# A four-stage graph network on one core: ScalarE's order in the plain layer, and the order and fusing of the last round

## The reference

```
# stage 1, "plain layer" (G = adjacency with multiplicities)
h = max(layernorm(x), 0)
t = (h + G h) W1 + b1;  t = relu(batch_norm(t));  x = x + relu(t W2 + b2)
h = max(layernorm(x), 0)                     # input of stage 2

# stage 3: h = max(layernorm(x),0) W_in + b_in, then four times (i = 0..3)
agg = norm * (G + I) (h Wc[i]) + bc[i]
y   = h + relu(agg)
mu  = mean(y);  var = mean((y - mu)^2)
h   = (y - mu) * rsqrt(var + 1e-5) * ln_g[i] + ln_b[i]
# after the fourth: out = x + h
```

## Time and profile before

| | |
|---|---|
| median of 3 runs | 2899.14 us (2898.2 to 2923.24) |
| span of the profiled execution, first to last instruction | 2555.2 us |
| plain layer, first to last sum matmul of its own | 1178.98 to about 1247 us |
| four last layers | about 2231 to 2544.8 us |
| last store issued | 2545.20 us |

### The profile page before, as it was taken

The page is one execution under the profiler, slowest core; times in us unless marked ns, Lnnn a source line. Parts: engine busy times, 40 slices in busy tenths (PEclk is TensorE's granted clock), DMA queues, the critical chain, the costliest instruction groups (busy, mean ns, idle before and its releaser), DMA issues.

```text
span 2555.2 us, 33445 instructions
## 1 busy us (share of the span) xinstructions
PE 1957.3 (77%) x11712; PEld 1075.9 (42%) x11712; DVE 1320.5 (52%) x3185; ACT 672.7 (26%) x1332; POOL 1480.3 (58%) x1529
## 2 busy tenths in 40 slices
PE   8855544554455544438999999999999999999996
PEld 4411111111111111125556555555555565577775
DVE  6576666666766666654322222222323333367775
ACT  4354454554445444424300000000000000100000
POOL 5477777777777777771166666664676667500000
PEclk8765565656565656568999999999999999999998
DMA  6655555555555555565454444445444444400000
GB/s 205 194 161 167 159 167 161 167 161 164 160 168 164 165 164 166 162 213 184 140 187 160 163 157 155 154 153 171 147 153 152 142 162 159 126 32 1 1 6 22
DMA packets 183330, 370.17 MB, mean 145 GB/s; under 512 B 38760, under 2 KB 119254, under 8 KB 174838
## 3 DMA queue, kind: packets, MB, share of 16 engines
q1 hardware_dynamic: 129208, 263.74, 29.1%
q0 software_dynamic: 48704, 101.21, 15.3%
q10 hardware_dynamic: 5246, 3.03, 0.4%
HBM read 232.54 MB, written 135.28 MB: 144 GB/s over the span
## 4 chain that ended last, share of the span: by engine, by line
PE 49%; DVE 3%; ACT 1%; issue 1%; DMA 0%; SPq 0%; ACTq 0%
PE ps_out L1910 26%; PE ps_out L1272 11%; PE ps_out L1890 6%; PE ps_out L1866 4%; PE ps_t L1343 1%; DMA bias<-in_L_gnn_ln_b 0%; DVE arena L1655 0%; PE ps_t L1840 0%; PE ps_out L1331 0%; PE ps_out L1880 0%; ACT H L875 0%; ACT H L882 0%; DVE H L1510 0%; DVE CS L1500 0%; DVE H L1511 0%
## 5 line engine op out<-in xcount | busy, mean ns | idle before, releaser
L946 POOL DMA_INDIRECT arena<-table_rel,key_rel x784 | 778.1, 992 | 245.5 <-issue 234.8
L1620 POOL DMA_INDIRECT arena<-table_cut,src_at x324 | 312.0, 963 | 256.2 <-DMA table_cut<-Z 103.2
L1063 PE MATMUL ps_t<-arena 128*128 128x50 f16 x1568 | 96.6, 213 | 462.1 <-DVE arena L975 462.1
L965 DVE SCALAR_TENSOR_TENSOR arena<-arena,keep_max 128x128 f32<-128x128 f32 x784 | 274.6, 350 | 322.6 <-DMA arena<-table_rel,key_rel 309.7
L1620 POOL DMA_INDIRECT arena<-table_next,src_at x324 | 315.5, 974 | 179.0 <-issue 91.8
L1128 ACT ACTIVATE arena<-ps_out 128x800 fp8e4<-128x800 f32 x512 | 399.9, 835 | 44.3 <-PE ps_out L1076 44.2
L1076 PE MATMUL ps_out<-arena 128*128 128x400 f16 x1024 | 375.0, 503 | 43.2 <-ACT arena L1128 43.2
L1910 PE MATMUL ps_out<-arena,Z 128*128 128x512 fp8e4 x1600 | 350.6, 379 | 0.9 <-DVE Z L868 0.9
L1910 PE MATMUL ps_out<-arena,cut 128*128 128x512 fp8e4 x1600 | 350.2, 379 | 0.0
L1063 PEld LDWEIGHTS ps_t<-arena 128*128 128x128 f16 x1568 | 79.2, 116 | 542.7 <-DVE arena L975 523.6
L981 DVE TENSOR_TENSOR arena<-iota,arena 128x1072 f16<-128x1072 f16 (+1 forms) x384 | 271.4, 707 | 0.0
(11 more groups left out here) (313 smaller groups left out, 2026.3 us busy)
## 6 DMA issues: line engine op xcount, KB each, us to landing
arena<-adjacency SPq DMA_DIRECT2D x64, 1600.0 KB, 6.9
adjacency<-arena SPq DMA_DIRECT2D x160, 320.0 KB
running_rows<-arena SPq DMA_DIRECT2D x392, 128.0 KB
arena<-adjacency_plain SPq DMA_DIRECT2D x50, 400.0 KB, 7.5
arena<-table_rel,key_rel POOLq DMA_INDIRECT x784, 2.9
table_rel<-arena SPq DMA_DIRECT2D x13, 512.0 KB, 3.9
adjacency_plain<-adj SPq DMA_DIRECT2D x50, 128.0 KB, 2.4
table_rel<-adj SPq DMA_DIRECT2D x12, 512.0 KB, 3.9
```

Of the source, the lines that this page charges most:

```text
L946: e.indirect_dma_start(message(g, t), None, table, bass.IndirectOffsetOnAxis(key[:, t:t + 1], 0)).then_inc(s_msg[t % both], 16)
L965: e.scalar_tensor_tensor(fold(t), fold(t - 1), g.keep_max[:, t:t + 1], message(g, t), ALU.add, ALU.max).then_inc(s_run, 1)
L1063: e.matmul(out[:, :, w * WIN:(w + 1) * WIN], g.hot_low[:, q % 2, w // 2, :, w % 2], g.hot_flat[:, q % 2, w // 2, :, w % 2].rearrange("p (a ...
L1620: e.indirect_dma_start(g.picked[:, w % 2 * BLOCKS + k, :, :].rearrange("p a f -> p (a f)"), None, tables[y], bass.IndirectOffsetOnAxis(g.s ...
```

## The change

1. In the plain layer ScalarE does `m.scalar` of rounds 0 and 1 first, then `norm.scalar` of rounds 0 and 1. Rounds 2 to 4 stay as they were.
2. In the last round of the last layer TensorE sums the three-tile part, then the first 6 of 25 source tiles (`AHEAD`) of the two-tile part, then multiplies the three-tile part by the weights, then sums the other 19 source tiles and multiplies the two-tile part.
3. In that round VectorE and ScalarE work on the three-tile part and on the two-tile part one after the other (`last_part`): ScalarE takes the squares of (y - mean) and their sums, and VectorE's centring, gain, scaling, shift and add to X become one fused operation per tile for (y - mean) * gain, one per tile for the scaling and the add to X, and one add of the shift to X ahead of both parts.
4. The last stores are three tiles after the first part, one tile and the 53 rows after the second.

```diff
@@ class Sums
+    def tensor_last(self, e, i, cut, weights, base):
+
+        n = base * (2 * TROUNDS)
+        e.wait_ge(self.s_z, n + (2 * i - 2))
+        e.sem_inc(self.s_go, 1)
+        self.add(e, i, 0, cut, range(NT), True, True).then_inc(self.s_sum, 1)
+        self.add(e, i, 1, cut, range(AHEAD), True, False)
+        self.product(e, i, 0, weights, n)
+        self.add(e, i, 1, cut, range(AHEAD, NT), False, True).then_inc(self.s_sum, 1)
+        self.product(e, i, 1, weights, n)
...
@@ isomorphism_layer
     def scalar(e):
         batch_norm_scalar(g, e, s_v, s_r)
-        for i in range(TROUNDS):
+        for i in range(EARLY_ROUNDS):
+            m.scalar(e, i, 1.0 / (scale * COUNT))
+        for i in range(EARLY_ROUNDS):
+            norm.scalar(e, i)
+        for i in range(EARLY_ROUNDS, TROUNDS):
             m.scalar(e, i, 1.0 / (scale * COUNT))
             norm.scalar(e, i)
@@ graph_layers, sync
-        for i in range(TROUNDS):
-            e.wait_ge(s_fin, i + 1)
-            lo, hi = i * TILES, min((i + 1) * TILES, NT - 1)
+        for done, lo, hi in [(r + 1, r * TILES, (r + 1) * TILES) for r in range(TROUNDS - 1)] + [
+                (TROUNDS + 2, NT - TILES, NT - 2), (TROUNDS + 4, NT - 2, NT - 1)]:
+            e.wait_ge(s_fin, done)
@@ graph_layers, vector
+        def last_part(q):
+
+            n, i, (lo, hi) = 3, TROUNDS - 1, m.parts[q]
+            at = slice(i * TILES + lo, i * TILES + hi)
+            y, h, var = g.Y[:, at, :], g.H[:, at, :], g.var[:, at]
+            e.wait_ge(m.s_prod, n * (2 * TROUNDS) + (2 * i + q + 1))
+            e.tensor_tensor(y, m.out(q).rearrange("p (k f) -> p k f", f=D),
+                            g.dis[:, at].unsqueeze(2).to_broadcast([P, hi - lo, D]), ALU.mult).then_inc(m.s_read, 1)
+            e.wait_ge(m.s_read, n * (2 * TROUNDS) + (2 * i + q + 1))
+            step(e.tensor_tensor(y, y, g.w9[:, (4 + n) * D:(5 + n) * D].unsqueeze(1).to_broadcast([P, hi - lo, D]), ALU.add))
+            step(e.scalar_tensor_tensor(y, y, 0.0, h, ALU.max, ALU.add))
+            step(e.tensor_reduce(g.mean[:, at], y, AX.X, ALU.add))
+            e.tensor_scalar(g.mean[:, at], g.mean[:, at], -1.0 / D, None, ALU.mult).then_inc(s_mean, 1)
+            e.wait_ge(s_mean, q + 1)
+            for k in range(at.start, at.stop):
+                e.scalar_tensor_tensor(g.H[:, k, :], g.Y[:, k, :], g.mean[:, k:k + 1], g.bias9[:, n * D:(n + 1) * D],
+                                       ALU.add, ALU.mult).then_inc(s_add, 1)
+            e.wait_ge(s_sq, hi)
+            e.tensor_scalar(var, var, 1.0 / D, 1e-5, ALU.mult, ALU.add).then_inc(s_v, 1)
+            e.wait_ge(s_r, ended + q + 1)
+            step(e.reciprocal(g.inv_dev[:, at], g.dev[:, at]))
+            e.wait_ge(s_add, hi + 1)
+            for k in range(at.start, at.stop):
+                e.scalar_tensor_tensor(g.X[:, k, :], g.H[:, k, :], g.inv_dev[:, k:k + 1], g.X[:, k, :],
+                                       ALU.mult, ALU.add).then_inc(s_fin, 1)
+
...
+                if n == 3 and i == TROUNDS - 1:
+                    tail = slice(i * TILES, NT)
+                    e.tensor_tensor(g.X[:, tail, :], g.X[:, tail, :], tall(g.bias9[:, (4 + n) * D:(5 + n) * D]),
+                                    ALU.add).then_inc(s_add, 1)
+                    e.wait_ge(s_add, 1)
+                    for q in range(2):
+                        last_part(q)
+                    continue
@@ graph_layers, scalar
+        def last_round(n, i):
+            m.mean(e, i, 0, g.inverse[:, n:n + 1], n)
+            squares(0)
+            m.mean(e, i, 1, g.inverse[:, n:n + 1], n)
+            deviation(0)
+            squares(1)
+            deviation(1)
```

More of the change, by code:

```diff
@@ L78 @@
 TILES = 5
+AHEAD = 6
 TROUNDS = NT // TILES
@@ L1324, in tensor, with mean, product @@
         self.products(e, i, weights, base)
+    def tensor_last(self, e, i, cut, weights, base):
[7 more added lines that the diff above has]
+        self.product(e, i, 1, weights, n)
+    def mean(self, e, i, q, inverse, base):
+        n, (lo, hi) = base * (2 * TROUNDS), self.parts[q]
+        e.wait_ge(self.s_prod, n + (2 * i - 2))
+        e.wait_ge(self.s_sum, n + (2 * i + q + 1))
+        e.sem_inc(self.s_go, 1)
+        e.activation(self.z[:, i % 2, lo * P:hi * P], self.sums(i, q), ACT.Copy, scale=inverse).then_inc(self.s_z, 1)
+    def product(self, e, i, q, weights, n):
+        lo, hi = self.parts[q]
+        e.wait_ge(self.s_z, n + (2 * i + q + 1))
+        e.wait_ge(self.s_read, n + (2 * i - 1 + q))
+        for k in range(lo, hi):
+            last = e.matmul(self.out(q)[:, (k - lo) * D:(k - lo + 1) * D], self.z[:, i % 2, k * P:(k + 1) * P],
+                            weights, start=k == lo, stop=k == hi - 1)
+        last.then_inc(self.s_prod, 1)
     def products(self, e, i, weights, base=0):
@@ L1456, in graph_layers @@
     s_c, s_v, s_r, s_fin, s_o = g.sem("gchain"), g.sem("gvar"), g.sem("gdev"), g.sem("gfinal"), g.sem("gout")
+    s_mean, s_sq, s_add = g.sem("gendmean"), g.sem("gendsquare"), g.sem("gendshift")
+    ended = 4 * TROUNDS - 1
     cuts = (g.zcut, g.cut)
@@ L1524, in scalar, with squares, deviation @@
     def scalar(e):
+        def squares(q):
+            lo, hi = m.parts[q]
+            e.wait_ge(s_mean, q + 1)
+            for k in range(lo, hi):
+                at = NT - TILES + k
+                e.activation(T[:, k, :], g.Y[:, at, :], ACT.Square, bias=g.mean[:, at:at + 1],
+                             accum_out=g.var[:, at:at + 1]).then_inc(s_sq, 1)
+        def deviation(q):
+            at = slice(NT - TILES + m.parts[q][0], NT - TILES + m.parts[q][1])
+            e.wait_ge(s_v, ended + q + 1)
+            e.activation(g.dev[:, at], g.var[:, at], ACT.Sqrt).then_inc(s_r, 1)
+        def last_round(n, i):
[5 more added lines that the diff above has]
+            deviation(1)
         def layer(n, x):
@@ L1527, in layer @@
                 at = slice(i * TILES, (i + 1) * TILES)
+                if n == 3 and i == TROUNDS - 1:
+                    last_round(n, i)
+                    continue
                 m.scalar(e, i, g.inverse[:, n:n + 1], base=n)
@@ L1548, in layer @@
                     e.wait_ge(s_last, 16 * TILES)
+                if n == 3 and i == TROUNDS - 1:
+                    m.tensor_last(e, i, cuts[x], g.w9[:, n * D:(n + 1) * D], n)
+                    continue
                 m.tensor(e, i, cuts[x], g.w9[:, n * D:(n + 1) * D], base=n, parts_of=parts_of if n else None)
```

## The result

| | before | changed |
|---|---|---|
| median of 10 runs each | 2899.22 us | 2884.88 us |
| lowest to highest | 2888.56 to 2923.24 | 2872.47 to 2897.81 |
| ratio | | 0.9954, 95% interval 0.9932 to 0.9975 |
| profiled execution: time, span | not given, 2555.2 | 2877.94, 2874.3 |

The change is worth 14.3 us at the medians, 7 to 20 us by the interval: within 1% of no change, and 1.1 us from the forecast of 2886.0.

The account below looks back on a forecast made before the run. Mostly TensorE bounds, idle behind ScalarE's order in the plain layer, with VectorE's chain alone at the end; 8.5 + 4.1 + 0.5 = 13.1 us off 2899.1 gave 2886.0 us, own range 2883 to 2889, wider range 2880 to 2896.

Parts of the forecast that it names:

- Edit 1, 8.5 us: Plain layer: ScalarE's earlier copies win 10.2 us, 1.7 us lost waiting for round 1's norm, 8.5 us carried to the end.
- Edits 2 to 4, the chain, 4.1 us: Last round: VectorE's chain in two parts issues the last stores at 2540.7 instead of 2544.79, 4.1 us earlier.
- upper bound of 4.4: Last round's chain: the most it was expected to gain, 4.4 us, by the price of the fused operations.
- The stores, 0.5 us: End of the kernel: last stores carry 192 KB less, at 406 GB/s worth 0.5 us.
- the bound of 2: Last stores: the most they could gain, about 2 us, if the 3.0 us wait were all bytes.
- The median lies 343.9 us above the span, which no edit touches: Whole kernel: the gain on the span of 2555.2 us was taken unchanged off the median of 2899.1 us.
- The sum: Whole kernel: 8.5 + 4.1 + 0.5 = 13.1 us off the span, time 2886.0 us.
- Given back at the boundary: Rival: the plain layer's lead is lost at the boundary to the next stage; 2894.5 us, 10 in 100.
- The clock falls: Rival: TensorE's clock drops at its pauses in the plain layer, costing 2.8 us; 2889 us, 10 in 100.
- the second of the two places: Plain layer, TensorE's 1.7 us without work at 1203.9; a clock fall there was to cost 2 us.
- the clock stays down: Slower rival: the lower clock holds through the plain layer's rounds 2 and 3; 2912 us, 2 in 100.
- The last round does not shorten: Rival: waits between ScalarE and VectorE in the last round eat the 4.1 us; 2890 us, 8 in 100.

Follow-up runs that it names:

- one-store kernel: Changed kernel, but tiles 20 to 23 stored by one 256 KB DMA at the end; last round still 20.36 us, wait for the stores 3.0 us.

## Why the prediction was right, point by point

- **What bounds.** Both places were read rightly: the pause of 8.15 us was ScalarE's order and nothing else (order alone, 8.4 to 8.5 us), and the end was VectorE's chain.
- **Edit 1, 8.5 us.** Measured 8.50 in the profile of the changed kernel. Its inner steps hold as well: no wait ahead of the second hidden product, none for adjacency; at round 2 TensorE pauses 1.45 us for ScalarE's norm, and the way from round 2's sums to round 3's is 1.7 us longer (said: 1.7), hence 8.5 and not 10.2.
- **Edits 2 to 4, the chain, 4.1 us.** Measured 4.66, which is above the upper bound of 4.4. The mechanism was right: VectorE decides the second part. For the fused form without a split 2.3 were forecast, with TensorE's old order; 1.8 were measured with the new one, and the old one would give about 2.5 (an estimate). The sizes were off in two terms. I let the root of the first part wait 0.3 us for ScalarE's copy; in the trace it starts at 2859.41, before the copy's 0.45 us from 2859.05 have passed, and the reciprocal's wait is the usual 0.28. The copy also started 0.2 us earlier in the round than I had it. And three fused operations took 0.80 us to the next start, not 0.96. Both terms lie in the first part, which also starts 0.1 us earlier: from the first sum to its end 16.17 us (2844.47 to 2860.64) where 16.72 were forecast (2519.74 to 2536.46); the second took 4.19, forecast 4.2.
- **The stores, 0.5 us.** Measured 0.9, by the wait and by the one-store kernel. The bytes at 406 GB/s were too small a price; the bound of 2 covered it.
- **"The median lies 343.9 us above the span, which no edit touches".** This step was wrong, though it cost the forecast nothing. Time and span of one execution of before differ by 1.7 to 1.9 us in each of the 75 that ran beside the timed experiments; the 344 us were the difference between an undisturbed chip and the one that the median came from. The sum held because the places that the change touches have the same lengths on all these chips (A 65.2 to 65.4 with the old order, 56.7 with the new, but for the clock's 1.7).
- **The sum.** 13.1 forecast, 8.5 + 5.6 = 14.1 by distances, 14.3 at the medians. The agreement of the last two is closer than the interval of 7 to 20 allows one to claim.
- **The rivals.** Given back at the boundary: no, 7.8 to 8.6 us arrive at the next stage's first store, and 8.8 to 11.7 at the last round. The clock falls: in one of the profiled executions with this order, at the second of the two places, at 1.7 us; never at the first. That the clock stays down: not seen. The last round does not shorten: no.

## What to carry to other kernels

When an engine idles for a result that was ready long ago, look at what stands ahead of the hand-over in the other engine's program; putting it where that engine waits anyway costs nothing, and the next thing that stands ahead tells how much of the gain is kept. Splitting the last chain pays only if the first part gets its input while the slower engine still works: the same split wins 2.8 us with the early product, and without it is 1.05 us worse than the form in one part, more if that one too has the old order. To price one edit of several, leave the others as they are on both sides. Where totals scatter by more than the effect, measure the distance between two events that enclose the change, and do not subtract a span of one chip from a time of another.

## What the runs showed that I had not expected

- **Where a set of runs fell decides more than the change.** The same kernel before took 2554 and 2556 us in two sets of runs (and its profile has that length), and 2899 to 2966 us in three others. In the latter the stage ahead of the plain layer and the one behind it were longer (1406 against 1179 us to the plain layer's first sum, and 1376.2 against 1270.1 from the next stage's first sum to the last round, changed kernel against before), with TensorE idle for ScalarE (398.9 of the 490.8 us above) and ScalarE, at the line that it waits for, idle for what the profile names "remote" (134.0 of 203.9 us, none of 44.3 before); the plain layer and the last round were not. Each set ran on one chip, so chip and moment are not told apart, and what causes it stays open.
- **Part of the shorter end does not reach the time.** Time less span is 1.7 to 1.9 us in every execution of before and of the kernel with only ScalarE's order. With the changed end it lies between 1.8 and 4.0, with medians from 2.0 to 3.6 (2.1 in the runs of the result): 0.2 to 1.8 us of the 5.6 are lost behind the last instruction. The size of the last store does not explain it: one execution with a store of 256 KB at the end has 3.6, and so has one with 64 KB. It was not settled.
- **The same pause, two clocks.** 1.45 to 1.50 us without a matmul left the granted clock at 1.00 in most executions and took it to 0.66 in a following stretch in one of eight.
- **Independent operations on ScalarE overlap here**: a root started 0.36 us after a copy of 0.45 us had.
